# Reordering the slots of the layers' loop, and turning the last tile's down rows one chunk later

## The reference

```python
h = x @ Win.T + bin                                   # 2048 x 64
for each of 4 layers:
    y = silu(layernorm(h))
    y = sconv(y)          # per channel: a geometric filter p**n over the tokens, p complex, real part kept
    h = h + y * sc_lin
    y = silu(layernorm(h) @ W1.T + b1) @ W2.T + b2    # 64 -> 256 -> 64
    h = h + y
x = layernorm(x + layernorm(h) @ Wout.T + bout)
Wg, Wu = codebook[idx_gate], codebook[idx_up]         # 1376 x 512, 8192 entries of 8 values
Wd = codebook[idx_down]                               # 512 x 1376
x = layernorm(x + (silu(x @ Wg.T) * (x @ Wu.T)) @ Wd.T)
```

## Time and profile before

| what | value |
|---|---|
| median of 3 runs | 1264.0 us (1263.94 to 1266.96) |
| profiled execution, its own time | 1264.5 us |
| its span | 1262.5 us |
| TensorE busy, mean granted clock | 1188.8 us (94%), 0.982 |
| VectorE busy | 1011.6 us (80%) |
| ScalarE busy | 261.7 us (21%) |
| GpSimd busy | 929.9 us (74%) |
| chain that ended last | GpSimd 73%, issue 21%, TensorE 4% |

### The profile page before, as it was taken

How to read it: one execution, slowest core, us unless ns; L and a number is a source line. 1 busy time by engine, 2 the same in 40 slices (tenths; PEclk the granted TensorE clock), 3 DMA queues, 4 the chain that set the end, 5 groups by cost and what they waited for, 6 DMA issues and landing times.

```text
span 1262.5 us, 16835 instructions
## 1 busy us (share of the span) xinstructions
PE 1188.8 (94%) x5595; PEld 839.3 (66%) x5595; DVE 1011.6 (80%) x2194; ACT 261.7 (21%) x395; POOL 929.9 (74%) x895
## 2 busy tenths in 40 slices
PE   6857998889999999999999999999999999999998
PEld 4533444346777777777777777777777777778876
DVE  3998898878997778888777888778888778888845
ACT  2325777772000000000000000000000000000024
POOL 6777777777777777777777777777777777777710
PEclk8968999989999999999999999999999999999999
DMA  9331211102433223433223433333433333334303
GB/s 202 64 68 37 45 37 39 27 4 53 105 92 87 65 71 80 95 82 92 65 69 79 89 85 81 65 70 86 93 85 87 67 70 79 94 72 88 60 2 133
DMA packets 96971, 93.57 MB, mean 74 GB/s; under 512 B 53549, under 2 KB 57909, under 8 KB 96886
## 3 DMA queue, kind: packets, MB, share of 16 engines
q1 hardware_dynamic: 64692, 83.86, 23.0%
q0 software_dynamic: 28160, 3.66, 8.5%
q10 hardware_dynamic: 4034, 4.98, 1.4%
HBM read 87.53 MB, written 4.90 MB: 73 GB/s over the span
## 4 chain that ended last, share of the span: by engine, by line
POOL 73%; issue 21%; PE 4%; DMA 1%; DVE 0%; ACT 0%; POOLq 0%; SPq 0%; DVEq 0%
POOL stage_down L400 57%; POOL stage_up L389 16%; PE bank L652 2%; PE cand L652 2%; DMA work<-in_L_ffn_idx_up 0%; DMA stage_down<-in_L_ffn_codebook,idx_down 0%; ACT x L505 0%; POOLq L160 0%; DVE chosen L1229 0%; DVE x L1033 0%; PE bank L924 0%; SPq L315 0%; DVE idx_low L1091 0%; DVE idx_low L1092 0%; DVE shift L1239 0%
## 5 line engine op out<-in xcount | busy, mean ns | idle before, releaser
L400 POOL DMA_INDIRECT stage_down<-in_L_ffn_codebook,idx_down x688 | 722.3, 1050 | 209.7 <-issue 209.1
L652 PE MATMUL cand<-one_hot,book 128*128 128x512 f32 (+1 forms) x2432 | 622.7, 398 | 19.0 <-DVE one_hot L1057 19.0
L1057 DVE TENSOR_SCALAR one_hot<-bc,low_of 128x512 fp32r<-128x512 uint16 (+1 forms) x1216 | 512.8, 482 | 99.0 <-PE cand L652 97.3
L652 PEld LDWEIGHTS cand<-one_hot,book 128*128 128x128 f32 x2432 | 449.7, 189 | 187.2 <-DVE one_hot L1057 51.8
L389 POOL DMA_INDIRECT stage_up<-in_L_ffn_codebook,idx_up x192 | 205.6, 1071 | 63.8 <-issue 58.2
L652 PE MATMUL bank<-x1t_hi,w 128*128 128x512 f32 (+1 forms) x704 | 239.1, 396 | 0.0
L1075 DVE SCALAR_TENSOR_TENSOR chosen<-bc,high_of,cand 128x512 f32<-128x512 uint16 (+1 forms) x304 | 220.2, 724 | 21.1 <-PE bank L652 17.9
L652 PEld LDWEIGHTS bank<-x1t_hi,w 128*128 128x128 f32 (+1 forms) x704 | 130.3, 185 | 31.4 <-issue 2.1
L652 PE MATMUL bank<-x1t_lo,w 128*128 128x512 f32 (+1 forms) x352 | 137.7, 391 | 0.0
L598 ACT ACTIVATE prod<-bank 128x512 f32<-128x512 f32 (+1 forms) x44 | 26.3, 599 | 389.4 <-PE bank L652 389.4
L605 ACT ACTIVATE act_hi<-prod 128x512 fp32r<-128x512 f32 x40 | 25.3, 633 | 342.5 <-DVE prod L1033 342.5
(11 more groups left out here) (181 smaller groups left out, 751.8 us busy)
## 6 DMA issues: line engine op xcount, KB each, us to landing
bc<-index_parts SPq DMA_DIRECT2D x272, 256.0 KB, 3.3
stage_down<-in_L_ffn_codebook,idx_down POOLq DMA_INDIRECT x688, 2.7
bc<-index_parts_rest SPq DMA_DIRECT2D x32, 192.0 KB, 3.1
x<-in_L_attn_x ACTq DMA_DIRECT2D x4, 1024.0 KB, 9.8
out_x<-x SPq DMA_DIRECT2D x16, 256.0 KB, 2.0
stage_up<-in_L_ffn_codebook,idx_up POOLq DMA_INDIRECT x192
index_parts<-parts_t SPq DMA_DIRECT2D x20, 32.0 KB, 2.0
w_in<-in_L_attn_W ACTq DMA_DIRECT2D x2, 256.0 KB
```

What stands on the lines that cost most here:

```text
L400: pool.indirect_dma_start(stage_down[k % RING][:, q, j * CS:(j + 1) * CS], None, a["L0_ffn_codebook"], bass.IndirectOffsetOnAxis(ap=idx_do ...
L652: return pe.matmul(dst, lhs, rhs, start=start, stop=stop)
L1057: done = v.tensor_scalar(one_hot[quad % 2][:, q, 0:nw], bc[quad % BCS][:, 0:nw], low_of[:, q:q + 1], None, ALU.is_equal)
```

## The change

In the layers' loop three engines' lists are reordered; no instruction is added or removed. On TensorE the first quad's candidates go to the head of the item, variance1 goes ahead of the mix, and the other candidates and the first add_up ahead of back. On VectorE the first one-hots go ahead of the mix's sum and the others behind it, and the choices stand ahead of add_back, silu's product and the scan. In the tail `turn_down(FULL, REST)`, `down_hi` and `down_lo` move from chunk 0 to chunk 1, and all down products and what follows them start one chunk of the loop later: the last two chunks of down products then have no hidden product between. ScalarE's out_chunk moves with them.

```diff
             for c in range(NC):
                 silu(FULL, REST, c)
                 product_hi(FULL, REST, c)
-                if c == 0:
+                if c == 1:
                     down_hi(FULL, REST)
-                if c >= 2:
-                    out_chunk(c - 2)
+                if c >= 3:
+                    out_chunk(c - 3)
+            out_chunk(NC - 3)
             out_chunk(NC - 2)
...
             for t in range(ITEMS):
                 quads = quads_in(t)
+                candidates(quads[0])
                 if t % NC:
 
                     pe.wait_ge(s["scanned"], t)
                     if t >= 3:
                         pe.wait_ge(s["ff_made"], t - 2)
                     mm(bank[2][:, 0:1], turn[:, t // NC, :], g[:, C - 1:C]).then_inc(s["rotated"], 1)
+                variance1(t)
                 if t:
                     mixed(t - 1)
-                variance1(t)
                 if t >= 2:
                     variance2(t - 2)
+                for quad in quads[1:]:
+                    candidates(quad)
+                add_up(quads[0] - 1)
                 if t >= 3:
                     back(t - 3)
-                candidates(quads[0])
                 if t >= 2:
                     spread(t - 2)
                 for quad in quads[1:]:
-                    candidates(quad)
-                for quad in quads:
                     add_up(quad - 1)
...
             add_up(ALL_QUADS - 1)
-            for c in range(NC + 1):
+            for c in range(NC + 2):
                 if c < NC:
                     hidden(FULL, REST, c, 0, 1)
-                if c == 0:
+                if c == 1:
                     turn_down(FULL, REST)
-                else:
-                    for t in range((c - 1) * TPC, c * TPC):
+                if c >= 2:
+                    for t in range((c - 2) * TPC, (c - 1) * TPC):
                         down(FULL, (FULL - 2, FULL - 1, FULL), t, (bank[2][:, :], cand[0][:, :], cand[1][:, :], cand[2][:, :]))
 
         @block.vector
...
                 if c:
                     v.wait_ge(s["rotated"], l * (NC - 1) + c)
                     v.tensor_copy(state[:, :], bank[2][:, 0:1]).then_inc(s["state_kept"], 1)
+                one_hots(quads[0] + 1)
                 if t:
                     add_mixed(t - 1)
-                one_hots(quads[0] + 1)
+                for quad in quads[1:]:
+                    one_hots(quad + 1)
                 v.wait_ge(s["rs1_made"], t + 1)
...
                 if t >= 2:
                     norm2(t - 2)
+                for quad in quads:
+                    choose(quad)
                 if t >= 3:
                     add_back(t - 3)
...
                 tt(d, g, tab[:, l, :], ALU.mult).then_inc(s["damped"], 1)
-                choose(quads[0])
-                for quad in quads[1:]:
-                    one_hots(quad + 1)
-                    choose(quad)
...
             last_pair = FULL // 2 - 1
-            for c in range(NC + 1):
+            for c in range(NC + 2):
                 if c < NC:
                     product(FULL, REST, c)
                     product_lo(FULL, REST, c)
-                if c == 0:
+                if c == 1:
                     down_lo(FULL, REST)
+                if c >= 3:
+                    make_shift((c - 3) * TPC, TPC, NT + c - 2)
                 if c >= 2:
-                    make_shift((c - 2) * TPC, TPC, NT + c - 1)
-                if c:
-                    for t in range((c - 1) * TPC, c * TPC):
+                    for t in range((c - 2) * TPC, (c - 1) * TPC):
                         add_down(last_pair, t, (bank[2][:, :], cand[0][:, :], cand[1][:, :], cand[2][:, :]))
```

## The result

The changed kernel takes 1271.8 us (median of 8 executions, 1267.0 to 1275.95); the kernel before, timed beside it, 1266.4 us (8 executions, 1263.94 to 1270.71). Ratio 1.0043, 95% interval 1.0026 to 1.0059: slower by some 5.4 us. The prediction said no change, 1264.4 us, with 1268.0 as its upper end, and was wrong. 2.4 us of the distance are the kernel before itself, whose median of three had been 1264.0.

A forecast was written before the change was run, and what follows sets the result against it. GpSimd's gather stream and a full TensorE were taken to bound the kernel, meeting at tile 7 and the end. Profiled 1264.5, +0.7 for the loop, -0.34 for the tail: 1264.9, median 0.5 lower, 1264.4 us; range 1261.3 to 1268.0.

The forecast's parts named there:

- TensorE's count for the loop: Layers' loop, items 3 to 15: TensorE needs 119.8 us of the 120.41 taken before; with waiting, a loss of 0.7.
- the prediction's 1.3 us of waiting: Items 3 to 15: TensorE's waiting left after the change, 0.1 us an item, where it waited 12.55 us before.
- The split pair's 13.65 us: Items 3 to 15: variances parted by the mix are each paid in full, +1.05 us of TensorE's time per item.
- The ring without TensorE: Plain loop item, scan to scan through turn, variances, mix, roots, table load, silu: 8.35 us, before 8.67.
- The first items ... I take -0.3: Loop's start up to the third scan: between +1.0 and -1.7 us, taken as a loss of 0.3.
- After the loop: After the last scan: the choice is out of the way of the last mix's sum, gain 0 to 0.6, taken 0.3 us.
- The cap at tile 7: Tile 7's down rows: TensorE's gain before 951 us beyond 0.4 us turns into a wait for GpSimd's gathers.
- The tail: Last tile's down rows turned a chunk later: TensorE's 0.34 us stand goes and the end moves by that.
- TensorE becomes the bound, slower: Rival, loop: split pair fills TensorE and each hand-over adds a wait; about 1269 us, chance 0.17.
- a second fall of the clock: Loop, within the TensorE-bound rival: another drop of TensorE's clock, priced at 1 us.
- The stream changes pace: Rival, GpSimd's gathers: VectorE's new order shifts their time by 1.8 us either way, felt at tile 7; chance 0.05.
- the prediction's own sign of being wrong: End of the gather stream: the last gather landing more than 2 us away from 1205.9 would show the prediction wrong.

The follow-up runs named there:

- pair_kept2: Changed kernel with the mix put ahead of both variances again, so the two stand side by side; ratio 1.0011 to the kernel before.
- before_warm_b: Kernel before, old order, with dummy products in TensorE's stands (22 ahead of the loop, then 14, 6, 4, 10); ratio 0.9983.
- early: Kernel before with half of the candidates' matmuls of quads 60 to 67 left out, 8 us of TensorE's work in tile 1's time; ratio 1.0012.
- after_warm2_b: Changed kernel, variances still split, with dummy products in TensorE's stands (22, 8, 8, 10, 10); ratio 0.9967 to the kernel before.
- pair_warm2: Changed kernel with the mix ahead of both variances and dummy products in TensorE's stands (22, 8, 8, 10, 10); 1262.1 us, ratio 0.9946.
- loop_only2: Kernel before with the changed loop alone, old tail kept; 1272.0 us, ratio 1.0027.
- tail_only2: Kernel before with the changed tail alone, old loop kept; 1267.0 us, ratio 1.0000.

## Why the prediction was wrong, step by step

- **TensorE's count for the loop: right for twelve of the thirteen items.** The two variances are groups of 2 records at 1.12 us around the mix, and the prediction's 1.3 us of waiting are the 1.3 us that the window shows. It gave a loss of 0.7 us for thirteen items; twelve of them gained 0.2, and the thirteenth, item 3, lost 3.13. From the third scan to the last TensorE was busy 122.03 of 123.34 us, where the count had 119.8: it took the half clock out of item 3, and item 3 had it again, to 121.3. A plain item takes 8.49 to 8.59 us from scan to scan (185.72, 194.31, 202.80), as said. The split pair's 13.65 us in thirteen items were 11.0 in twelve. (The Trainium skill, TensorEngine Tiling (Array Packing), section Key Properties, says that different tiles can load weights and multiply in parallel. The trace agrees: two side by side last 1.13 us, one alone 1.12.)
- **The ring without TensorE: too short.** The prediction had it at 8.35 us for a plain item with the pair split, and so would have given the whole pair as a gain to a kernel that keeps it. pair_kept2 shows 3.5 us: its plain items take 8.43 (TensorE busy 7.70 of them, VectorE 7.59). The term was right in TensorE's time and far too large as a price.
- **"The first items ... I take -0.3": the step that failed.** It is a loss of 0.3 us up to the third scan, with 1.7 as its bound; measured were 3.3 us there and 6.4 at the fourth scan. The first scan came at 99.17 where 97.9 to 98.9 was said, but in part by luck: the clock was full again from 94.0 (97.9 was said for that), and the second quad's candidates and choice, about 1 us, were not in the sum. The sentence that the candidates stood on the second scan's path anyway was 2.3 us off. For the third scan I had 112.9 to 113.9 and 1.7 more if the clock falls; it came at 117.25, with the clock at half from 107.7 to 121.3. And I didn't walk item 3 at all but counted it as a plain one: turn behind the candidates (2.3 us after the scan's end), stage_up and adder ahead of back. The diff shows that move, and the prediction's list of the parts has only candidates, variance and choices.
- **After the loop: wrong in sign.** I gave 0.3 us for the choice that is out of the way, and the mix comes no sooner after the scan (2.06 us against 2.07). And I did not ask what TensorE does while it waits for the last scan, now that its candidates are done: 2.71 us of nothing, and 3.2 us of half clock behind it. 1.04 us lost.
- **The cap at tile 7: right that it exists, wrong that it is fixed.** In before_warm_b and early TensorE stood there for the gathers, and the stand also cost the clock behind it. But the prediction took its place, 951, and its 0.4 us of room from one trace. The changed loop itself brought the last of those gathers 4.9 us sooner, and after_warm2_b and pair_warm2 gain 3.9 and 7.9 us against before on their chips, far more than 0.4. (That trace was also one of the quick executions of the kernel before, 1264.5 us where its medians are 1266.4 to 1270.0; a slower one comes later to tile 7 and has more room.) With the changed kernel 7.2 us late at tile 7, no part of its loss is the cap's.
- **The tail: right, and worth nothing here.** No stand, 16 us between the last gather's landing (by 1202.0) and the turning, 0.6 us in the trace against 0.34 said, nothing in the time. The old tail takes as long where TensorE is late (81.80 us in loop_only2).
- **The rivals.** "TensorE becomes the bound, slower" named about this time (1269) at 0.17, but by waits in the steady items, and there are none: that it came near is luck. Its half sentence on "a second fall of the clock" was priced at 1 us; the clock's part of the loss is nearer 3. "The stream changes pace" came true at more than twice its price (4.9 us at tile 7 and 3.9 at the last gather, against 1.8), against the expectation that the sum would stay; it also fired the prediction's own sign of being wrong, a last gather over 2 us away. No one felt it in the changed kernel, TensorE being late.
- **Of the 7.3 us at tile 0's rows**, the traces put some 4 to 5 at the order of the first items and some 3 at the half clock that the changed kernel has more of (1.7 for 3.5 us of it in the first items, and the 1.0 lost after the loop, where it has 3.2 us more). That is an estimate from single executions. The medians don't confirm it: the same order with the dummies measures 0.9967 and the old order with them 0.9983, a difference inside both intervals and of the other sign, for the old order loses its lead of 5.3 us to half clock from 262.3 to 272.5 and to the meeting at tile 7. What is shown is that the loss arises in the loop's first items and behind its last, that the order loses 3.7 to 5.3 us up to the last scan with little half clock in either kernel, and that 3.4 us of half clock cost 1.64. How much of each the median's 5.4 us hold is not settled.

## What to carry to other kernels

Walk a reordered loop's first and last items one by one, with every product that moves, not only its steady item: here the steady items came out to 0.2 us, and the ends lost 7.5. When an order leaves a hole on TensorE, price what may run behind the hole at half clock, not only the hole. And before counting a gain, look for the next place where another stream arrives at about the same time, and read that stream's pace in more than one trace: 8 us of work taken away in front of it gave nothing, and its place moved by 9.7 us between kernels that all issue the same gathers.

## What the runs showed of the hardware

- A stand of 2.02 us on TensorE that was otherwise full was followed by granted clock 0.50 (in the windows of 952 to 955), one of 2.25 us in the loop's start by 0.50 from 107.7 to 121.3, in which TensorE stood once more, for 1.57 us. (The Trainium skill, TensorE: Matmul & The Clock Gate, section Loop structure matters more than you think, says that whether matmuls stay warm is set by the loop nest, and its example of what breaks it is an 8 us wait for a DMA. In this case the clock also fell behind waits of 2.02 and 2.25 us.)
- Dummy products in the stands raised the changed kernel's mean clock from 0.979 to 0.989 and took 0.76% off its time. They did not hold the clock up everywhere: with the same dummies pair_warm2 fell to 0.50 at 109.5 and at 263, and before_warm_b at 262.3.
- The same instructions at the same place got half clock in one execution and not in another: behind the same stand of 1.46 us tail_only2 had 3.4 us of it, for 1.64 us of time, and before had none. The stretch from the last scan to tile 0's rows took 67.03 us in the one profile with no half clock in it and 70.2 to 75.0 in the twelve others.
- A gather of the down rows took 2.29, 2.33 and 3.54 us to land, and the last of all 880 started between 1198.8 and 1207.9 in thirteen profiles, with the pauses ahead of the down rows' gathers all but unchanged (209.6 to 209.8 us): the mean of one of these gathers went from 1043 to 1055 ns.
